# Layer 2 of a graph network: row gathers replaced by counted meetings of tiles and target blocks

## What is computed

```python
tgt, nbr = edge_index[0], edge_index[1]          # src, dst
agg_sum = segment_sum(x[nbr], tgt, num_segments=n)
deg = segment_sum(ones(E), tgt, num_segments=n)
agg = agg_sum / maximum(deg, 1.0)[:, None]
out = relu(x @ Wl + bl + agg @ Wr + br)
out = out / (norm(out, axis=1) + 1e-06)
```

## Time and profile before

| | us |
|---|---|
| runs of the kernel before | 13067.85, 13086.51, 13090.25 |
| median | 13086.51 |
| span of the profiled execution | 13042.0 |
| `l2_edges`, first gather to last add | 2499.6 |

### The profile page before, as it was taken

One profiled execution on the slowest core, in us unless ns is written; L12 is line 12 of the kernel. 1 busy time (PEld: TensorE's weight loads), 2 busy tenths in 40 slices (PEclk: granted clock), 3 DMA queues, 4 the chain that ended last, 5 costly groups with the idle time before them and its releaser, 6 DMA issues. The chain is left out here.

```text
span 13042.0 us, 141627 instructions
## 1 busy us (share of the span) xinstructions
PE 6959.8 (53%) x39559; PEld 6176.4 (47%) x39560; DVE 5953.9 (46%) x15920; ACT 2034.5 (16%) x3901; POOL 6815.9 (52%) x6934
## 2 busy tenths in 40 slices
PE   0033333333566477777777433333333678888886
PEld 0033333333566455555555322222223677777775
DVE  8822222222577655555555322222225455555555
ACT  4011111111455511111111100000000000000000
POOL 0066666666100166666666366666662666566663
PEclk5566666666787788888888655555556555555555
DMA  3044444444444344444444511111113233333335
GB/s 132 30 128 128 128 127 128 127 128 128 127 112 114 103 120 123 124 123 120 124 119 123 97 47 47 46 48 48 46 47 44 74 82 86 82 86 83 87 85 83
DMA packets 1209335, 1250.67 MB, mean 96 GB/s; under 512 B 265745, under 2 KB 992358, under 8 KB 1209018
## 3 DMA queue, kind: packets, MB, share of 16 engines
q0 software_dynamic: 248832, 577.29, 17.7%
q1 hardware_dynamic: 954266, 668.17, 17.7%
q10 hardware_dynamic: 6048, 2.84, 0.1%
HBM read 842.78 MB, written 404.91 MB: 96 GB/s over the span
## 5 line engine op out<-in xcount | busy, mean ns | idle before, releaser
L984 POOL DMA_INDIRECT buf<-node_rows,buf x3456 | 3369.8, 975 | 2057.4 <-issue 1485.9
L1478 POOL DMA_INDIRECT buf<-node_rows_ln,buf x1728 | 1746.8, 1011 | 1032.7 <-DVE buf L1605 545.7
L650 POOL DMA_INDIRECT edge_rows_by_src<-buf x1728 | 1690.8, 978 | 1042.8 <-ACT buf L660 525.6
L998 PE MATMUL psum<-buf 128*128 128x129 f32 x3456 | 780.3, 374 | 1754.3 <-issue 1305.1
L694 PE MATMUL psum<-buf 128*128 x3456 | 722.4, 375 | 1676.7 <-ACT buf L669 990.4
L998 PEld LDWEIGHTS psum<-buf 128*128 128x128 f32 x3456 | 685.4, 281 | 1849.2 <-issue 1484.4
L694 PEld LDWEIGHTS psum<-buf 128*128 128x128 f32 x3456 | 651.3, 280 | 1732.5 <-issue 1732.3
L1008 DVE TENSOR_TENSOR agg<-agg,psum 128x129 f32 x864 | 250.4, 290 | 1860.2 <-DMA agg<-running_sums 1697.0
L2157 PE MATMUL psum<-buf 128*128 128x132 f32 x3456 | 872.7, 413 | 358.5 <-issue 344.1
L2157 PEld LDWEIGHTS psum<-buf 128*128 128x128 f32 x3456 | 764.9, 309 | 442.9 <-issue 441.8
L2149 PE MATMUL psum<-buf 128*128 128x5 f32 x3456 | 752.9, 355 | 116.3 <-ACT buf L2126 87.2
(11 more groups left out here) (340 smaller groups left out, 12067.8 us busy)
## 6 DMA issues: line engine op xcount, KB each, us to landing
buf<-edge_rows_by_src SPq DMA_DIRECT2D x114, 1056.0 KB, 5.7
buf<-edge_rows_by_src SPq DMA_DIRECT2D x110, 1024.0 KB
buf<-in_edge_attr SPq DMA_DIRECT2D x864, 128.0 KB
running_weighted_sums<-buf SPq DMA_DIRECT2D x108, 544.0 KB
buf<-loc_rows_by_src SPq DMA_DIRECT2D x110, 512.0 KB
buf<-loc_rows_by_dst SPq DMA_DIRECT2D x110, 512.0 KB
running_sums<-buf SPq DMA_DIRECT2D x108, 512.0 KB
buf<-node_rows,buf POOLq DMA_INDIRECT x3456
```

What stands on the lines that cost most here:

```text
L650: nc.gpsimd.indirect_dma_start(rows, bass.IndirectOffsetOnAxis(ap=at[:, h, t:t + 1], axis=0), st[:, h, t, :], None).then_inc(scattered[h], 16)
L984: nc.gpsimd.indirect_dma_start(rows[:, t, 0:used], None, table, bass.IndirectOffsetOnAxis(ap=stage[:, t:t + 1], axis=0)).then_inc(sem, 16)
L998: last = nc.tensor.matmul(ps[:, q // 3, (q % 3) * W:(q % 3) * W + width], oh[:, 2 * q + s, :], rows[:, 2 * q + s, 0:width], start=(s == 0) ...
L1478: nc.gpsimd.indirect_dma_start(xn[:, j, t, :], None, table1, bass.IndirectOffsetOnAxis(ap=stage[:, j // 4, at:at + 1], axis=0)).then_inc(g ...
```

## The change

`l2_edges` gathers nothing any more. A *meeting* is a pair of one tile of edges and one block of 128 targets in which the tile has at least one edge (a tile's edges are sorted by `dst`, so it meets a run of neighbouring blocks). For a meeting PE multiplies two one-hot matrices in bf16, the edge's target within the block and its source within its block, contracted over the 128 edges. The product counts the edges between each target and each source. PE then multiplies it by the block's 128 rows, split into three bf16 parts whose sum is the float32 row, and accumulates 8 meetings (`IG`) of one block of sources in PSUM. `NMEET = 4512` meetings are always worked off, the empty ones among them.

- `l2_lists` is new: it transposes `idx` and `loc` into a DRAM table of one row per tile, counts the meetings of each tile, places them by scans, scatters each tile's first meeting into a DRAM list (14 indirect DMAs), and reads it back, works out each meeting's tile, target block and source block, gathers the tiles' rows (36 indirect DMAs) and transposes them into `ends_of` (bf16).
- `l2_nodes` stores no rows; it splits them into `parts` (bf16).
- `l2_edges` is new but for its name: DVE compares 16 tiles at once, twice per unit of 16 meetings; PE builds and applies; ACT moves the counts from PSUM as bf16; DVE adds one block for each 8 meetings.
- `rank_phase` gets a third query between POOL, PE and ACT, and the branch `sort_by_dst`, entered only when `dst` isn't sorted, a longer body.

```diff
+IG = 8
+NMEET = 4512
+NJ = 4608
+JR = NJ // P
+TPP = NTX // P
+XW = 3 * D + 2
...
             l1_finish(nc, c, ins, table1, running, last_pairs)
-            l2_nodes(nc, c)
-            l2_edges(nc, c, blk_a)
+            with nc.sbuf_tensor([P, 2, NJ], BF16) as ends_of, nc.sbuf_tensor([1, NJ], I32) as dst_blk, nc.sbuf_tensor([1, NJ // IG], I32) as src_blk:
+                l2_lists(nc, c, qtab, tile_rows, starts, meet_rows, ends_of, dst_blk, src_blk)
+                with nc.sbuf_tensor([P, NB, XW], BF16) as parts:
+                    l2_nodes(nc, c, parts)
+                    l2_edges(nc, c, ends_of, dst_blk, src_blk, parts)
             l2_finish(nc, c, ins)
...
-                for k in range(2):
+                for k in range(3):
                     act.wait_ge(answered, k + 1)
...
+def l2_lists(nc, c, qtab, tile_rows, starts, meet_rows, ends_of, dst_blk, src_blk):
...
+                sp.wait_ge(kept, QC)
+                sp.dma_start(tile_rows.rearrange("(p r) k -> p (r k)", p=P), rows[:].rearrange("p r k -> p (r k)")).then_inc(rows_out, 16)
+                sp.wait_ge(scattered, 16 * TPP)
+                sp.dma_start(st[:], starts.rearrange("(a b) w -> a b w", a=JR)).then_inc(starts_in, 16)
...
+                pool.wait_ge(offered, 1)
+                for r in range(TPP):
+                    nc.gpsimd.indirect_dma_start(starts, bass.IndirectOffsetOnAxis(ap=at[:, r:r + 1], axis=0), values[:, r, :], None).then_inc(scattered, 16)
+                pool.wait_ge(known, 1)
+                pool.sem_inc(gathering, 1)
+                for k in range(JR):
+                    nc.gpsimd.indirect_dma_start(gath(k).rearrange("p k e -> p (k e)"), None, tile_rows, bass.IndirectOffsetOnAxis(ap=tile_of[:, k:k + 1], axis=0)).then_inc(got[k // KG], 16)
...
+                for g in range(JR // KG):
+                    dve.wait_ge(got[g], 16 * KG)
+                    part = gath(g * KG, KG)[:, :, 0:P]
+                    nc.vector.tensor_tensor(part, part, bc(lift_of[:, g * KG:(g + 1) * KG].unsqueeze(2), [P, KG, P]), ALU.subtract).then_inc(lowered, 1)
...
+def l2_nodes(nc, c, parts):
...
-            @block.sync
-            def _(sp):
-                sp.wait_ge(filled, 1)
-                for first in range(0, NB, KB * 2):
-                    end = min(first + KB * 2, NB)
-                    sp.wait_ge(rectified, end)
-                    sp.dma_start(rows[:, first:end], tab[:, first:end, :]).then_inc(stored, 16)
-                sp.wait_ge(stored, 16 * -(-NB // (KB * 2)))
...
+                for g, (first, count) in enumerate(GROUPS):
+                    for b in range(first, first + count):
+                        last = nc.scalar.activation(f[:, b, :], c["x"][:, b, :], ACT.Relu, bias=st.nmr[:, b:b + 1], scale=st.rstd[:, b:b + 1])
+                    last.then_inc(raised, 1)
+                for g, (first, count) in enumerate(GROUPS):
+                    act.wait_ge(left, g + 1)
+                    nc.scalar.copy(middle[:, first:first + count], rest[:, first:first + count]).then_inc(lowered, 1)
...
+                for g, (first, count) in enumerate(GROUPS):
+                    of = slice(first, first + count)
+                    dve.wait_ge(raised, g + 1)
+                    ch.link(nc.vector.tensor_copy(high[:, of], f[:, of]))
+                    nc.vector.tensor_tensor(rest[:, of], f[:, of], high[:, of], ALU.subtract).then_inc(left, 1)
+                for g, (first, count) in enumerate(GROUPS):
+                    of = slice(first, first + count)
+                    dve.wait_ge(lowered, g + 1)
+                    nc.vector.tensor_tensor(low[:, of], rest[:, of], middle[:, of], ALU.subtract)
...
+def l2_edges(nc, c, ends_of, dst_blk, src_blk, parts):
...
-            @block.gpsimd
-            def _(pool):
-                for h in range(R):
...
             @block.scalar
             def _(act):
...
+                act.sem_inc(moved, 2)
+                with act.Fori(0, NMEET // (UNITS * U)) as i:
+                    for h in range(2 * UNITS):
+                        g = 2 * UNITS * i + h
+                        act.wait_ge(built, g + 1)
+                        act.wait_ge(summed, g + 1)
+                        nc.scalar.copy(meets[:, h % 2].rearrange("p a k -> p (a k)"), psM[:, h % 2].rearrange("p a k -> p (a k)")).then_inc(moved, 1)
...
             @block.tensor
             def _(pe):
...
+                def build(g, h, u):
+                    if h % 2 == 0:
+                        pe.wait_ge(hot, u + 1)
+                    pe.wait_ge(moved, g + 1)
+                    for k in range(IG):
+                        at = IG * (h % 2) + k
+                        last = nc.tensor.matmul(psM[:, h % 2, k, :], hot_dst[:, (h // 2) % 2, at, :], hot_src[:, (h // 2) % 2, at, :], start=True, stop=True)
+                    last.then_inc(built, 1)
+
+                def apply(g, h, i):
+                    blocks = nc.values_load_multi_w_load_instructions(
+                        dst_blk[0:1, bass.ds(2 * UNITS * IG * i + IG * h, IG)], engines=[ENG.PE], min_val=0, max_val=NB - 1,
+                        skip_runtime_bounds_check_because=BLOCK_RANGE)[1]
+                    pe.wait_ge(moved, g + 3)
+                    pe.wait_ge(added, g + 1)
+                    for k in range(IG):
+                        rows = flat(parts[:, bass.ds(blocks[k], 1), :])
+                        for a, (lo, n) in enumerate(((0, D + 2), (D + 2, D), (2 * D + 2, D))):
+                            last = nc.tensor.matmul(psO[:, h % 2, 0:n], meets[:, h % 2, k, :], rows[:, lo:lo + n], start=(k == 0 and a == 0), stop=(k == IG - 1 and a == 2))
+                    last.then_inc(summed, 1)
+
+                pe.sem_inc(summed, 2)
+                build(0, 0, 0)
+                with pe.Fori(0, NMEET // (UNITS * U)) as i:
+                    for h in range(2 * UNITS):
+                        g = 2 * UNITS * i + h
+                        build(g + 1, h + 1, UNITS * i + (h + 1) // 2)
+                        apply(g, h, i)
...
             @block.vector
             def _(dve):
...
+                def hot_of(u, b, at):
+                    for to, w in ((hot_dst, 0), (hot_src, 1)):
+                        last = nc.vector.tensor_tensor(to[:, b], bc(iota[:].unsqueeze(1), [P, U, P]),
+                                                       bc(ends_of[:, w, at].unsqueeze(2), [P, U, P]), ALU.is_equal)
                     last.then_inc(hot, 1)
...
+                def add(g, h, block):
+                    dve.wait_ge(summed, g + 3)
+                    dve.wait_ge(added, g + 2)
+                    a = flat(agg[:, bass.ds(block, 1), 0:D + 1])
+                    nc.vector.tensor_tensor(a, a, psO[:, h % 2, 0:D + 1], ALU.add).then_inc(added, 1)
+
+                dve.sem_inc(added, 1)
                 nc.vector.memset(agg[:], 0.0).then_inc(added, 1)
...
+                nc.vector.tensor_copy(iota[:], c["iota"][:]).then_inc(numbered, 1)
+                dve.wait_ge(numbered, 1)
+                hot_of(0, 0, slice(0, U))
+                with dve.Fori(0, NMEET // (UNITS * U)) as i:
+                    blocks = nc.values_load_multi_w_load_instructions(
+                        src_blk[0:1, bass.ds(2 * UNITS * i, 2 * UNITS)], engines=[ENG.DVE], min_val=0, max_val=NB - 1,
+                        skip_runtime_bounds_check_because=BLOCK_RANGE)[1]
+                    for h in range(2 * UNITS):
+                        g = 2 * UNITS * i + h
+                        if h % 2 == 0:
+                            u = UNITS * i + h // 2
+                            dve.wait_ge(built, 2 * u)
+                            hot_of(u + 1, (h // 2 + 1) % 2, bass.ds(UNITS * U * i + U * (h // 2 + 1), U))
+                        add(g, h, blocks[h])
```

More of the change, by code:

```diff
@@ L126, in gnn_kernel @@
     running = dram("running_sums", (P, NPAIR + 1, D))
+    tile_rows = dram("tile_rows_by_src", (NTX, 2 * P))
+    starts = dram("first_meetings", (NJ, 2))
+    meet_rows = dram("blocks_of_meetings", (2, NJ), I32)
     with es:
@@ L419, in _ @@
                     sort_by_dst(ch.n)
-                pool.sem_inc(asked, 2)
+                pool.sem_inc(asked, 3)
             @block.tensor
@@ L1706, in l2_nodes @@
     f = tab[:, :, 0:D]
+    high, middle, low = (parts[:, :, k:k + D] for k in (0, D + 2, 2 * D + 2))
     with es:
-        st = NodeStats(sb, sem)
-        dve_chain, stats, rectified, filled, stored = (sem() for _ in range(5))
-        rows = c["table"].rearrange("(b p) w -> p b w", p=P)
+        st, rest = NodeStats(sb, sem), sb([P, NB, D])
+        dve_chain, stats, raised, left, lowered = (sem() for _ in range(5))
         with nc.Block() as block:
-            @block.sync
-            def _(sp):
-                sp.wait_ge(filled, 1)
-                for first in range(0, NB, KB * 2):
-                    end = min(first + KB * 2, NB)
-                    sp.wait_ge(rectified, end)
```

(38 more changed lines are left out.)

240 lines of the change are left out of this document (202 added, 38 removed).

## The result

The changed kernel takes 13381.80 us (median of four runs, 13376.42 to 13388.23); the kernel before, run beside it, takes 13088.38 (13067.85 to 13091.95). The ratio is 1.0232, 95% interval [1.0218, 1.0245]: slower by 2.3%. The span of the profiled execution is 13374.6 us, 332.6 more than before.

The account below looks back on a forecast made before the run. POOL's issue of gathers was taken to bound the old stage. Span 13042.0 + loop 158 + lists 110 + nodes 5 + rank phase 2 = 13317; + 44.5 = 13,361, stated as 13,360 us; range 13,050 to 13,780.

Parts of the forecast that it names:

- comparisons: DVE's two comparisons of 2048 elements per unit in the new loop, forecast at 4.48 us.
- build, block numbers, waits, up to the apply: PE's eight product matmuls, 0.40 us, then reading eight block numbers, 0.75, and waits, 0.10, per unit.
- apply, with the last result: PE's 24 matmuls on the chain, each with its own address operation: 103 ns each, 2.47 us, plus 0.22 latency.
- add with its hand-over: DVE's add on the chain after the apply: 0.43 us plus 0.07 hand-over, 0.50 per unit.
- way back: DVE's read of four block numbers at the loop head, once per two units: 0.45 us per unit.
- closed chain: New loop: comparisons, build, apply, add wait for one another through DVE's and PE's in-order queues; 9.37 us a unit.
- fast rival: DVE comparisons run at double rate, 2.3 us a pair, so PE sets the unit: 12,863 us; 12 in 100.
- slow rival: PE's read of eight block numbers takes 1.936 us, making the unit 10.72 and the kernel 13,743 us; 15 in 100.
- equal rival: The three parts' apply matmuls share an address operation: 62 ns each, unit 8.39 us, kernel 13,087 us; 10 in 100.
- Lists: The new list-building stage, a chain through all engines with nothing beside it: about +110 us, from 85 to 150.
- Nodes: The node stage: removed row store saves 5 us, casts and subtractions add about 9; forecast +5 us.
- the ring's turns: Old loop: POOL idles about 6 us at each turn of the four-buffer gather ring, the rest beyond 2160 us of issue.

Follow-up runs that it names:

- e3: Changed kernel with only the dst comparison left in the loop, the src one made once ahead; loop 2420.9 us against 2715.0.
- e1: Changed kernel with the adds into agg moved one comparison later, all work kept; loop 2418.7 us against 2715.0, ratio 1.0294 to the kernel before.
- e11: Changed kernel without the third part's matmuls, 16 apply matmuls per group in place of 24; loop 2427.6 us against 2715.0.
- e5: Changed kernel with adds one comparison later and two apply matmuls per meeting in place of three; loop 1924.2 us, ratio 0.9846 to the kernel before.
- e9: e5 with six units in a loop body in place of two; loop 1901.4 us, ratio 0.982 to the kernel before.
- e2: Changed kernel with a meeting's three apply matmuls reading the same columns, so one register address serves all three; loop 2458.1 us against 2715.0.
- e7: The changed kernel unaltered, run on another chip; loop 2714.9 us, ratio 1.0549 to the kernel before there.
- e8: The kernel before, unaltered, traced on another chip; its old layer-2 edge stage took 2208.1 us, not 2499.6.
- e4: Changed kernel with one 386-column apply matmul per meeting in place of three, and three adds per group; loop 2775.9 us against 2715.0.
- e6: Changed kernel with adds one comparison later, one 386-column matmul per meeting and three adds per group; loop 2028.5 us, ratio 0.9942 to the kernel before.
- e12: e9 with DVE's block numbers read two at a time behind each unit's comparisons; loop 1792.1 us, ratio 0.9543 to the kernel before.

## Why the prediction came out right, and where it was off

The forecast was 13,360 us, the result 13381.8. The mechanism was right, and the smallness of the miss is partly luck. By spans, 13317 was forecast and 13374.6 measured, 57.6 short: the loop took 57 more than its 2658, the lists 4 less, and what lies outside layer 2 grew by 6.8 in place of 2. Against that, I added the 44.5 us that lay between the profiled span of before and its median, and after the change this is 7.2. In nearly every other run on record the device time is 1.8 to 1.9 us above its own span (2.1 in e3), so most of the 44.5 was not time around the span: the profiled execution of before was some 24 us faster than the fastest of the three timed runs. Profiled executions scatter like others, and a distance taken from one of them is not a constant.

The steps, in us per unit, read from the timeline above:

| step | forecast | measured |
|---|---|---|
| comparisons | 4.48 | 4.49 |
| build, block numbers, waits, up to the apply | 1.25 | 1.13 |
| apply, with the last result | 2.47 + 0.22 | 3.25 and 3.16, mean 3.21 |
| add with its hand-over | 0.50 | 0.43 |
| way back | 0.45 | -0.06 and 0.70, mean 0.32 |
| unit | 9.37 | 9.58 (9.57 over the loop) |

- **The closed chain** is what e1, e3 and e11 show: opening it gives 296 us back, shortening DVE's link the same and no more, and eight matmuls count once per unit.
- **The comparisons** ran at 2289 ns against 2286 of L1181. The fast rival, double rate, falls. The Trainium skill was split on it: the trace agrees with "Vector Engine (DVE) Microarchitecture Reference", section 5.1, and not with the 1224 ns of "VectorE: DVE Perf Modes", the tier table.
- **The block numbers** took 0.592 us as in L1049; the slow rival, 1.936 us, falls. e5 and e9 suggest what made L1506 slow: where the read starts.
- **The apply is the term that was mis-sized**, by 0.5 us a unit. I split L1119's 142 ns per two matmuls and one address operation evenly, and so put a matmul with its own operation at 99 ns. It costs 127: what a second matmul under the same operation adds is less than I gave it, and the first more. The stretch of L1119 that I read shows it: from 4017.5 us on its weight loads start 15 ns apart within a pair, and 118 ns or more from the second of a pair to the next. L1528, 0.82 us for six with one lasting 0.273, was the nearer row, with the same operation per matmul; I cited its 110 ns and then took a value below it. My upper end of 2.74 didn't hold the 3.0 measured. The clock, from which I made that upper end, is not what sets it.
- **The equal rival**, a shared operation, isn't what the kernel does (13536 operations); e2, which makes it so, gets 8.66 us a unit, above the 8.39 that I gave it, since some applies ran at half clock (2.49 us against 1.39).
- **The way back and the add** were 0.2 too dear together. Their numbers had been taken from a read of eight; this head reads four, in 0.346 us.
- **Lists**: 105.8 against 110, with the gathers of 1 KB rows paced at 1.26 us as assumed. **Nodes**: +4.6 against +5 (though the 9 and 5 of the prediction make +4). The **rank phase**'s +2 fits: the stage behind it starts 1.8 us later (603.9 against 602.1). The rest of the 11.3 us ahead of layer 2 I didn't foresee. The traces of e7 and e8 show 8.9 there (6381.9 against 6373.0); its cause is open.
- **What I left out** is the other side of the sum. The 2499.6 us of the old loop held a wait for data that the trace of e8 doesn't have. I named the ring's turns, but took them as a fixed part of the stage; and not each turn waits: the trace of before has 44 such stands, 264.6 us in all. On the chip of e7 the same change is a loss of 612 us, outside my range in ratio (1.0549 against 13,780 / 13,086.5 = 1.053).

## What to carry to other kernels

Before totals, write down the order on each in-order queue: a kernel can be bound by a closed chain in which no engine is busy, and moving one consumer behind the next producer's work (e1) opens it without any work added or removed. Here a matmul with an address operation of its own was priced by that operation (127 ns; 58 with one for three, e2), so fewer, wider ones pay, but only once the chain is open and the array stays busy (e4 against e5 and e6). Put register reads behind a long operation already in flight (e12), and keep in mind that the distance between a stage bound by landing data and one bound by issue can change from chip to chip: old and new loop are 215 us apart on the first chip and 507 on that of e7.

## What the runs showed of the hardware

- A stream of matmuls of 128 to 130 columns, each with its own address operation, takes 127 to 128 ns per matmul at both granted clocks; where every other one has 258 columns, they follow each other 128 ns apart at 2.4 GHz (e5). With one operation for three it takes 58 ns at 2.4 GHz and 104 at 1.2 GHz (e2).
- VectorE's reads of index lists: 4 numbers 0.346 us and 12 numbers 0.849 where the read starts at a multiple of four; 0.965 and 2.725 where it starts one number later. That the start is the reason is not shown.
- After PE had stood for most of 4.4 us in e4, the next eight matmuls of 386 columns ran at a granted clock of 0.50 (2.75 us) and the eight after them at 1.00 (1.48 us).
- In two sets of runs the kernel before took 13088 and 13248 us, in three others, on other chips, 11202 to 11234. The four stages of 1728 indirect DMAs differ (2475 to 2815 us each in the first trace, 2170 to 2273 in e8); the new loop, without transfers, takes 2715.0 and 2714.9.
